# Indirect transfers without a bound for their indices, in a kernel with a recurrence and an expert layer

## The reference

```python
xn = _layernorm(x, axis=-1)
s = _L0_attn_ref(xn, ...)        # W_in, a gated scan over 8 state columns, W_out
g = _silu(_L0_ffn_ref(xn, ...))  # the expert branch
x = x + s * g
```

```python
fe = idx.reshape(-1)                       # 8192 * 4 choices of an expert
pos = (jnp.cumsum(oh, axis=0) * oh).sum(-1) - 1
keep = pos < cap                           # cap = 1280
dest = jnp.where(keep, fe * cap + pos, E * cap)
buf_tok = jnp.full((E * cap + 1,), N, jnp.int32).at[dest].set(tok)[:-1]  # unfilled rows: token N
xe = xp[buf_tok].reshape(E, cap, DIM)      # xp has a zero row for token N
h = jax.nn.silu(jnp.einsum('ecd,edh->ech', xe, w1)) * jnp.einsum('ecd,edh->ech', xe, w3)
out = jnp.einsum('ech,ehd->ecd', h, w2) * buf_w.reshape(E, cap, 1)
y = jnp.zeros((N + 1, DIM), x.dtype).at[buf_tok].add(out.reshape(E * cap, DIM))[:N]
z = jax.nn.silu(xf @ sw1) * (xf @ sw3) @ sw2   # one expert that all tokens share
return (y + z).reshape(shape)
```

## Time and profile before

| | |
|---|---|
| median of 3 runs | 1098.25 us (1097.14 to 1103.78) |
| span of the profiled execution | 1097.6 us |
| PE busy | 972.7 us, 89% |
| DVE busy | 791.3 us, 72% |
| POOL busy | 729.7 us, 66% |
| ACT busy | 584.1 us, 53% |
| transfers | 190.20 MB, mean 173 GB/s |

### The profile page before, as it was taken

How to read it: one execution, slowest core, us unless ns; L and a number is a source line. 1 busy time by engine, 2 the same in 40 slices (tenths; PEclk the granted TensorE clock), 3 DMA queues, 4 the chain that set the end, 5 groups by cost and what they waited for, 6 DMA issues and landing times.

```text
span 1097.6 us, 29588 instructions
## 1 busy us (share of the span) xinstructions
PE 972.7 (89%) x7998; PEld 947.0 (86%) x7998; DVE 791.3 (72%) x2551; ACT 584.1 (53%) x1114; POOL 729.7 (66%) x571
## 2 busy tenths in 40 slices
PE   5878888888888899999999999999999999999910
PEld 4777777777888789999999999999999999999900
DVE  6666876887787777776777677777667777777786
ACT  4757767877888444444444444444444444444442
POOL 1066777777777766757776666666775676767745
PEclk8789999999999999999999999999999999999955
DMA  9933433334334788888787787788788798888699
GB/s 283 307 124 124 146 138 128 139 134 143 140 141 145 219 220 177 161 177 159 153 160 156 159 182 165 149 158 196 155 151 183 153 186 162 177 183 151 111 282 358
DMA packets 169413, 190.20 MB, mean 173 GB/s; under 512 B 19546, under 2 KB 161155, under 8 KB 169347
## 3 DMA queue, kind: packets, MB, share of 16 engines
q0 software_dynamic: 53312, 71.50, 35.9%
q1 hardware_dynamic: 115408, 117.91, 35.6%
q10 hardware_dynamic: 626, 0.01, 0.0%
HBM read 87.21 MB, written 105.79 MB: 176 GB/s over the span
## 4 chain that ended last, share of the span: by engine, by line
PE 69%; issue 9%; DVE 7%; ACT 5%; DMA 5%; POOL 2%; SPq 1%; DVEq 0%; POOLq 0%; ACTq 0%
PE h L781 13%; PE h L783 13%; PE h L782 13%; PE yb L801 7%; PE yb L799 7%; PE yb L800 7%; PE xt L765 6%; POOL y_sum L650 1%; ACT rows L1014 1%; DMA y_sum<-y_more,y_idx 1%; DMA slot_rows<-rows 1%; DVE act L1323 1%; POOL slot_rows L679 1%; PE gb L859 1%; SPq L424 1%
## 5 line engine op out<-in xcount | busy, mean ns | idle before, releaser
L650 POOL DMA_INDIRECT y_sum<-y_more,y_idx x220 | 349.8, 1590 | 193.3 <-issue 146.3
L781 PE MATMUL h<-xh,w_hl 128*128 (+1 forms) x1392 | 411.5, 296 | 3.3 <-DVE xl L1317 2.0
L783 PE MATMUL h<-xl,w_hl 128*128 (+1 forms) x1392 | 396.4, 285 | 0.0
L782 PE MATMUL h<-xh,w_hl 128*128 (+1 forms) x1392 | 395.0, 284 | 0.0
L679 POOL DMA_INDIRECT slot_rows<-rows,dest_idx x256 | 253.2, 989 | 117.1 <-issue 72.6
L1087 ACT ACTIVATE acth<-act 128x512 fp32r<-128x512 f32 x174 | 109.7, 631 | 318.4 <-PE yb L801 300.2
L781 PEld LDWEIGHTS h<-xh,w_hl 128*128 128x128 f32 x1392 | 266.1, 191 | 5.4 <-issue 4.3
L782 PEld LDWEIGHTS h<-xh,w_hl 128*128 128x128 f32 x1392 | 266.5, 191 | 0.0
L783 PEld LDWEIGHTS h<-xl,w_hl 128*128 128x128 f32 x1392 | 266.5, 191 | 0.0
L1327 DVE TENSOR_TENSOR actl<-act,acth 128x512 fp32r<-128x512 f32 x174 | 120.6, 693 | 181.6 <-ACT acth L1087 181.4
L799 PE MATMUL yb<-w_hl,acth 128*128 128x256 f32 x696 | 197.8, 284 | 5.0 <-DVE y_more L1583 2.7
(11 more groups left out here) (215 smaller groups left out, 1395.3 us busy)
## 6 DMA issues: line engine op xcount, KB each, us to landing
rows<-slot_rows SPq DMA_DIRECT2D x143, 289.0 KB, 5.0
raw<-L_ffn_w SPq DMA_DIRECT2D x99, 256.0 KB
slot_rows<-rows SPq DMA_DIRECT2D x47, 289.0 KB, 4.0
x_all<-L_attn_x SPq DMA_DIRECT2D x16, 512.0 KB, 6.6
out<-s_all SPq DMA_DIRECT2D x32, 256.0 KB, 5.5
y_sum<-yw SPq DMA_DIRECT2D x31, 256.0 KB
slot_rows<-rows,dest_idx POOLq DMA_INDIRECT x256
y_sum<-y_more,y_idx POOLq DMA_INDIRECT x220, 5.4
```

Source lines behind the costliest of these rows:

```text
L650: pool.indirect_dma_start(y_dram, bass.IndirectOffsetOnAxis(y_idx[:, buf, t:t + 1], 0), y_out[buf][:, t, :], None, bounds_check=token_boun ...
L781: mm(out, high, xh[:, k, cols], start=(k == 0), stop=False)
L782: mm(out, low, xh[:, k, cols], start=False, stop=False)
L783: ins = mm(out, high, xl[:, k, cols], start=False, stop=(k == KD - 1))
```

## The change

The indirect transfers lose `bounds_check` and `oob_is_err`. What the bound left out has to go somewhere, so both tables grow: `slot_rows` from 49152 to 122880 rows (65536 + 49152 + 8192) and `y_sum` from 8192 to 65792 rows (65536 + 256). The zero rows' column `TOK` holds, in place of one number for all, `FAR` plus a number from 0 to 255, so that the 256 rows of a block have 256 different targets behind row 65536 of `y_sum`. Nobody reads these rows. To write that column POOL executes an iota in place of a memset (L629), and DVE, which writes the zero rows a second time behind phase A (`zeros_again`), a tensor_scalar on the token numbers in place of a memset. The two registers with the bounds go.

```diff
-        slot_rows = nc.dram_tensor("slot_rows", (E * STRIDE, ROW), F32).ap()
-        y_dram = nc.dram_tensor("y_sum", (N, D), F32).ap()
+        slot_rows = nc.dram_tensor("slot_rows", (int(FAR) + E * STRIDE + N, ROW), F32).ap()
+        y_dram = nc.dram_tensor("y_sum", (int(FAR) + 2 * P, D), F32).ap()
...
-            sp.dma_start(y_dram[(A_PAIRS - 1) * PAIR:, :].rearrange("(t p) c -> p t c", p=P),
+            sp.dma_start(y_dram[(A_PAIRS - 1) * PAIR:N, :].rearrange("(t p) c -> p t c", p=P),
                          last_z[:, :, :]).then_inc(last_z_stored, 16)
...
-            pool.memset(zero_rows[:, :, TOK:TOK + 1], FAR).then_inc(zero_ready, 1)
-            slot_bound = pool.to_reg(E * STRIDE - 1)
-            token_bound = pool.to_reg(N - 1)
+            pool.iota(zero_rows[:, :, TOK:TOK + 1], [[P, 2]], int(FAR), 1, allow_small_or_imprecise_dtypes=True
+                      ).then_inc(zero_ready, 1)
...
                     pool.indirect_dma_start(
                         y_dram, bass.IndirectOffsetOnAxis(y_idx[:, buf, t:t + 1], 0), y_out[buf][:, t, :], None,
-                        bounds_check=token_bound, oob_is_err=False, compute_op=ALU.add).then_inc(added[buf], 16)
+                        compute_op=ALU.add).then_inc(added[buf], 16)
...
                         pool.indirect_dma_start(
                             slot_rows, bass.IndirectOffsetOnAxis(dest_idx[slot][:, t, k:k + 1], 0),
-                            rows[slot][:, t, :], None, bounds_check=slot_bound, oob_is_err=False
-                        ).then_inc(scattered[slot], 16)
+                            rows[slot][:, t, :], None).then_inc(scattered[slot], 16)
...
-                v.memset(zero_rows[:, :, TOK:TOK + 1], FAR).then_inc(zero_ready, 1)
+                v.tensor_scalar(zero_rows[:, :, TOK], token[:, 0:2], FAR, None, ALU.add).then_inc(zero_ready, 1)
```

## The result

The changed kernel takes 1115.17 us (median of 4 runs, 1114.56 to 1117.5), the kernel before 1097.7 us (median of 4, with one run more than the three shown above). The ratio is 1.0161, 95% interval 1.0135 to 1.0187: 1.6% slower, 17.5 us. The forecast was 1094.4 us and its range ended at 1109 us. The execution with the profile took 1114.56 us, 1.9 us more than its span of 1112.7 us.

A forecast was written before the change was run, and what follows sets the result against it. POOL's unbroken chain of adds, level with PE, was taken to set the end; its -20 us (shorter adds, +8 for sent rows) was capped at 2.6 + 0.8, plus 0.4 at the start: 3.8 us gained, 1094.4 us, range 1089 to 1109.

The forecast's parts named there:

- 2.6 us at the last yw: Limit on POOL's gain: its send of the last yw could move from 1039.16 to 1036.57 us, then waits for DVE.
- Part 1: POOL's time to generate an indirect transfer: without the check 0.10 us less for an add, half that for a scatter.
- the same floor: Point where POOL catches up with DVE; any add saving over 0.04 us reaches it, gaining 2.6 us at the last yw.
- Part 2: Left-out rows are now sent, lengthening landing waits behind yw's adds: 6.5 to 9.9 us on POOL's chain, taken 8.
- The six sections: Sections whose second add of yw sent nothing before: waits 1.08 us longer each, 6.5 us in all.
- the seven: Sections whose second add of yw sent under a fifth of its rows: 0.49 us more each, 3.4 us in all.
- the others: Remaining expert sections, used as the comparison for the waits; no added time was forecast for them.
- Part 3: The rest: iota, tensor_scalar and longer tables cost zero; shorter scatters gain 0.4 us before the expert phase.
- 0.4 us at the start: PE's 0.39 us wait for the expert phase's first rows goes, as scatters ahead get 0.05 us shorter.
- Rival 1: The check costs no time, so only the sent rows count: 1106.3 us; chance 0.29 together with savings below 0.04 us.
- rival 2: The 284 adds generate slower without a bound: over 1% from 0.01 us each, 1120 us at +0.05; 0.15 with Rival 3.
- Rival 3: Adds wait on the 256 shared targets: 1 us more in each of 30 sections, 1136 us; 0.15 with rival 2.

The follow-up runs named there:

- f1: Kernel before with two small POOL memsets, each waited for, behind each section's landing wait: 1122.54 us, 1.0199.
- f2: Kernel before with a bound of 0 on yw's adds, leaving out the sums of each expert's last pair: 1095.94 us, 0.9963.
- e1: Changed kernel with both bounds back but set behind the far rows, so nothing is left out: 1116.3 us, 1.0147.
- e4: Kernel before with the two longer tables and nothing else changed: 1098.43 us, 0.9991.
- e2: Changed kernel with the old bound back on the 64 adds of yw only: 1098.13 us, 0.9978.
- e3: Kernel before with the bound taken off the 256 scatters alone and slot_rows longer: 1097.92 us, 0.9996.
- e5: Kernel before with one small POOL memset and its wait behind each section's landing wait, on a slower chip: 1215.08 us, 1.0102.
- e8: Kernel before with yw's adds at bound 0 (last pairs' sums left out) plus one POOL memset per section, slower chip: 1214.61 us, 1.0067.
- e7: Changed kernel with short tables, zero rows' targets right behind row 8191, on a slower chip: 1225.38 us, 1.0211.
- e6: Kernel before with a bound of 0 on yw's adds (last pairs' sums left out), on a slower chip: 1209.11 us, 1.0013.

## Why the prediction was wrong

**The reading of the kernel held.** PE and POOL run at one pace, the page's 66% for POOL hides a chain without a gap, and a microsecond on it is one at the end: the 15.3 us in the trace and f1 show it. That POOL could win only 2.6 us at the last yw came out in f2. The pages' own chains of the work that ended last, before and changed, would have misled here:

```profile
PE 69%; issue 9%; DVE 7%; ACT 5%; DMA 5%; POOL 2%; SPq 1%; DVEq 0%; POOLq 0%; ACTq 0%
PE 34%; issue 19%; POOL 15%; DMA 14%; DVE 9%; ACT 6%; POOLq 2%; DVEq 0%; ACTq 0%; SPq 0%
```

Before the change the view followed PE and gave POOL 2%. It follows one chain, and of two that keep the same pace it names one; only in the changed kernel, where PE waits for buffers, does POOL's come out.

**The step that failed is Part 1**, the estimate that an add gets 0.10 us shorter without the check. It got 0.010 us longer (1554 to 1564 ns), and a scatter 0.003 us shorter and not 0.05. The estimate came from no row: the range of bounds was wide on both sides, and "work that is no longer asked for can go" took a value from the middle of one side. The rows that the step itself cites spoke for no change: no add took under 1537 ns, whether it sent all of its rows or none. Since any saving over 0.04 us led to the same floor, the choice between "some saving" and "none" carried the whole forecast, and I gave "some" 0.56. With a saving of 28 us in the sum the sign of POOL's account was wrong, and the floor was never reached.

The section of the Trainium skill that I weighed there (DMA: Bandwidth & Descriptors, "SWDGE vs HWDGE vs iDMA") says that a program makes the descriptors of these transfers; the runs show no part of its time that goes with the bound: 1554 ns with a bound that leaves rows out, 1554 with one that leaves none out (e1), 1564 without.

**Part 2 had the right mechanism and too small a size**: 8 us were taken, 13.8 us measured in the trace. The six sections were given 6.5 us and have 5.6; the seven were given up to 3.4 us and have 6.4; the others were given nothing and have 1.8. Over the kernel before, the changed one and e1 to e4 (two that send the rows, four that don't) the mean waits are 4.30 against 3.40 us in the six, 4.76 against 3.95 in the seven, and 4.48 against 4.26 in the other 17, which is 5.4, 5.7 and 3.7 us. The seven were read as if their first adds' rows made their waits about as long as a full section's: the difference of 0.49 us between groups of sections in one trace mixed the rows sent with what else differed between these sections. With and without the rows, the same sections of either group differ by 0.8 to 0.9 us. Nor are the 17 all alike: in eight of them at most 32 of yw's 256 rows were left out, and their wait grows by 0.15 us (4.25 to 4.40); so the more rows were left out, the more the wait grows. The 0.3 us for 131 KB that the prediction estimated from the Trainium skill (DMA: Bandwidth & Descriptors, section "Anatomy of one DMA — SWDGE (gpsimd) path") are a third of the 0.9 us of the six, in which the first add of yw sends left-out rows as well; the measurement decides.

**Part 3 held** in that the tables, the iota and the scatters cost nothing (e2, e3, e4). Its 0.4 us at the start did not come: the scatters were not shorter by 0.05 us, and PE's wait for the first rows is 0.45 us in place of 0.39:

```profile
379.02 0.66 PE L763 MATMUL xt<-ident,rows 128*128 128x128 f32 x4 [0.45 <-DMA rows<-slot_rows]
```

**The rivals.** Rival 1, that the check costs no time, was the right one in kind: 1106.3 us, range to 1109. The 1115.17 us lie 9 us above its centre: 5.8 are the size of Part 2, and the rest is within what two executions differ by, with up to 2.7 of it from the 10 ns. PE's waits for buffers that it foresaw are there. Its upper end left out the seventeen sections that I had called unchanged, and any longer generation. The 10 ns are rival 2 with its price at its own threshold (0.01 us), but not its mechanism: bounded adds get them too (e3). Rival 3, shared targets, fell: in the kernels that send the zero rows, the eight sections whose two adds of yw carry nearly only real rows have waits as long as the six in which at least 128 rows go to shared targets (4.40 and 4.30 us), and the last add's start needs no such term.

## What to carry to other kernels

An engine with a third of its time idle can still be the bound: lay its instructions side by side with those that it takes from, and see whether any lag ever shrinks to a wait. What an index bound saves is not the time to make the transfer, which is the same for a left-out row, but the row's way through the queue, so rows at the end of a list that something waits for should be left out. When all of the outcome hangs on a cost that no row shows, take the rows' own hint ("the same whatever is sent") as the forecast, and size a wait's change by the same place with and without the rows, not by other places.

## What the runs showed of the hardware

- POOL takes as long for an add whose rows are all left out as for a full one (at least 1537 ns and 1554 in the median, before), and a packet of a left-out row took a DMA engine some 8 ns, that of a sent one some 140 (before and changed kernel, about 446 us).
- An add with a bound takes 10 ns more (1554 to 1564 or 1565) when another indirect transfer of the same program has none (e2, e3), an add without a bound takes the same 1564 (changed kernel), and scatters don't show it (972 before, 969 changed). Why stays open.
- A landing wait grows with the rows that the adds ahead of it send: by 0.9 us with at least 128 of 256 rows more, by 0.15 us with at most 32 more (means over two kernels that send them and four that don't).
- POOL starts an add 0.98 us behind the memset that it waits for, and a memset 0.15 us behind (f1).
- On one chip the part ahead of the expert phase took 92 to 101 us longer for each of four kernels (e5 to e8), at a mean granted clock of 0.85 to 0.86 against 0.95, and the expert phase some 12 us longer (e7 700.2 against 688.1 us, e6 680.3 against f2's 668.2).
